# A graph attention block: crossings of the score matrices by memory instead of by TensorE

## The reference

```
u = h @ h.T / sqrt(384)                       # scores, 128 x 128, symmetric
a = softmax(u) * adjacency
attn = a / (sum(a) + 1e-10)
ctx = upper(attn) @ (h @ Wl.T + bl) + diag(attn) * (h @ Ws.T + bs) + lower(attn) @ (h @ Wr.T + br)
h = relu((ctx - mean) / sqrt(var + 1e-12) * ln_w + ln_b)
# after both layers
out = layernorm(x + h)
```

## Time and profile before

| | |
|---|---|
| median of 3 | 1630.99 us (1630.69 to 1631.91) |
| the profiled execution | 1631.82 us, of it the span of instructions 1630.1 us |
| granted TensorE clock | 0.997 of full speed |
| busy: TensorE, VectorE, GpSimd, ScalarE | 98%, 86%, 74%, 66% |
| matmuls | 9509, of them 6912 for projections, 1536 for gathers, 768 for score parts, 256 cross matmuls |
| moved by transfers | 179.17 MB, 110 GB/s |

### The profile page before, as it was taken

One profiled execution on the slowest core, in us unless ns is written; L12 is line 12 of the kernel. 1 busy time (PEld: TensorE's weight loads), 2 busy tenths in 40 slices (PEclk: granted clock), 3 DMA queues, 4 the chain that ended last, 5 costly groups with the idle time before them and its releaser, 6 DMA issues.

```text
span 1630.1 us, 35740 instructions
## 1 busy us (share of the span) xinstructions
PE 1605.1 (98%) x9509; PEld 1597.9 (98%) x9509; DVE 1398.9 (86%) x4368; ACT 1078.0 (66%) x2835; POOL 1212.5 (74%) x1542
## 2 busy tenths in 40 slices
PE   8999999999999999999999999999999999999996
PEld 7899999999999999999999999999999999999995
DVE  7788888888888888888888888888888888888886
ACT  6566666666666666666666666666666666666654
POOL 5677777777777777777777777777777777777764
PEclk9999999999999999999999999999999999999998
DMA  5444444444444444444444444444444444444431
GB/s 175 102 110 107 114 114 107 111 107 116 107 114 111 110 107 113 114 107 112 107 115 106 114 112 110 109 110 115 107 114 109 112 106 114 114 108 111 108 93 45
DMA packets 463943, 179.17 MB, mean 110 GB/s; under 512 B 348592, under 2 KB 462896, under 8 KB 463920
## 3 DMA queue, kind: packets, MB, share of 16 engines
q1 hardware_dynamic: 463920, 178.91, 43.3%
HBM read 112.92 MB, written 65.86 MB: 110 GB/s over the span
## 4 chain that ended last, share of the span: by engine, by line
PE 92%; DMA 1%; DVE 1%; SPq 1%; POOL 1%; ACT 1%; issue 1%; DVEq 0%; POOLq 0%; ACTq 0%
PE p_proj L430 70%; PE p_gather L517 16%; PE p_score L424 5%; PE p_score L446 1%; DMA rows_mem<-rows_blocks 1%; SPq L366 1%; DMA attnT_whole<-attn_mem 1%; SPq L351 0%; POOL rstd L1173 0%; POOL attnT L1163 0%; DVE stats L623 0%; POOL attnT_split L1169 0%; DVE p_gather L646 0%; DVE p_gather L619 0%; DVE rows_blocks L725 0%
## 5 line engine op out<-in xcount | busy, mean ns | idle before, releaser
L430 PE MATMUL p_proj<-w,hT_layer 128*128 128x384 f32 x6912 | 1368.6, 339 | 0.9 <-DVE w L744 0.5
L430 PEld LDWEIGHTS p_proj<-w,hT_layer 128*128 128x128 f32 x6912 | 1162.5, 188 | 2.0 <-POOL w L1220 1.0
L281 POOL TENSOR_TENSOR proj_split<-proj,proj_split 128x768 fp32r<-128x768 f32 x253 | 467.6, 1848 | 182.3 <-ACT proj_split L943 181.9
L517 PE MATMUL p_gather<-proj_split,attnT_split 128*128 128x384 f32 x1536 | 309.3, 335 | 2.3 <-POOL attnT_split L1169 1.6
L1173 POOL TENSOR_TENSOR rstd<-veps,neg_half 128x1 f32<-128x1 f32 x384 | 206.8, 549 | 91.9 <-DVE veps L632 82.6
L517 PEld LDWEIGHTS p_gather<-proj_split,attnT_split 128*128 128x128 f32 x1536 | 269.9, 188 | 4.7 <-POOL attnT_split L1169 2.7
L943 ACT ACTIVATE proj_split<-proj 128x768 fp32r<-128x768 f32 x256 | 214.9, 839 | 84.7 <-DVE proj L688 83.7
L688 DVE TENSOR_TENSOR proj<-p_proj,bias_all 128x768 f32<-128x768 f32 x256 | 244.9, 957 | 12.9 <-PE p_proj L430 5.1
L1169 POOL TENSOR_TENSOR attnT_split<-attnT,attnT_split 128x256 fp32r<-128x256 f32 x256 | 190.3, 743 | 71.0 <-ACT attnT_split L934 70.9
L947 ACT ACTIVATE o<-y,nbias,rstd 128x384 f32<-128x384 f32 x128 | 90.7, 709 | 227.0 <-POOL nbias L1177 227.0
L424 PE MATMUL p_score<-hT_layer 128*128 128x256 f32 x768 | 216.6, 283 | 1.8 <-DVE rows L720 0.8
(11 more groups left out here) (59 smaller groups left out, 1598.3 us busy)
## 6 DMA issues: line engine op xcount, KB each, us to landing
xt_raw<-xT SPq DMA_DIRECT2D x128, 192.0 KB, 2.6
xn<-x SPq DMA_DIRECT2D x128, 192.0 KB, 2.4
out<-o SPq DMA_DIRECT2D x128, 192.0 KB, 2.0
rows_mem<-rows_blocks SPq DMA_DIRECT2D x124, 192.0 KB, 1.9
rowsT<-rows_mem SPq DMA_DIRECT2D x496, 48.0 KB, 2.4
adj_layer<-adj SPq DMA_DIRECT2D x256, 64.0 KB, 1.9
attn_mem<-attn_blocks SPq DMA_DIRECT2D x124, 128.0 KB, 1.7
attnT_whole<-attn_mem SPq DMA_DIRECT2D x496, 32.0 KB, 2.2
```

Of the source, the lines that this page charges most:

```text
L281: op.tensor_tensor(proj_split[u][:, LO], proj[u][:, UP:LOW + 1, :], proj_split[u][:, HI].bitcast(F32), ALU.subtract).then_inc(s_proj_lo[k], 1)
L430: return nc.tensor.matmul(p_proj[:, which, 0:D], hT_of(k, b)[:, slot, st, c, :], w[:, k, which, mv, c, :], start=(n == 0), stop=(n == 8))
L517: last = nc.tensor.matmul(home(k, b)[:, 0:D], AT_split[u][:, st, side, :], proj_split[u][:, mv, side, :], start=(side == UP and n == 0), s ...
```

## The change

It has four parts.

1. In the loop the cross matmuls are gone. H and X of both layers are computed in one group, `pair_slice`, within `project_self(0, i)`: for graph i+2 of layer 1 and graph i-2 of layer 2. All four parts share one PSUM bank. ScalarE copies both X to SBUF in one instruction (`copy_cross`) and both H to places that are left in other banks (`keep_high`), so that the bank is free for the next pass. Layer 1's high and low input therefore has four slots instead of two, and the input is loaded a pass earlier.
2. X is transposed with the attention's trip: VectorE's `turn_cross` transposes the blocks of both X into planes 2 and 3 of `blocks`, and the trip (`store_swap`, `load_swap`) carries four planes instead of two. GpSimd adds X and its transpose (`add_cross`), right behind `attn_arrived`.
3. VectorE's `scaled_scores` take the kept H and that sum. They stand right behind `low_rows`, with a wait for `s_cross_sum` and `s_kept`, and the masks come behind layer 1's bias. The gather of layer 2 comes after the first four matmuls of layer 2's sides instead of before them. On SyncE the residual input comes ahead of `store_rows`, layer 2's adjacency behind `load_swap`.
4. The ends: graph 5's scores of layer 1 come in pass 3, with a cross matmul; graph 2's rows are transposed by TensorE; the output's mean, sum and deviation have two slots instead of one, and the last `output_squares` comes a pass earlier. In filling and closing passes the cross matmuls remain, 11 in all, as against 256 before.

The core of the diff, indented less, with empty lines left out:

```diff
+parts = [p_score[0][:, 0:2, :], p_score[0][:, 2:4, :]]
+cross_parts = p_score[0].rearrange("p (k t) n -> p k t n", t=2)[:, :, LO, :]
+E = [p_score[1][:, 0, :], p_score[1][:, 1, :]]
 p_rows = bank("p_rows", [P, 4, N])
-ident_p = [p_score[0][:, 3, :], p_score[1][:, 3, :]]
-attn_mem = [nc.dram_tensor(f"attn_mem_{slot}", (P, 2, N), F32, kind="Internal").ap() for slot in range(2)]
+ident_p = p_score[1][:, 2, :]
+kept = [p_rows[:, 3, :], p_gather[0][:, D:D + N]]
...
-def store_attn(i, slot):
-    first, last = attn_layers(i)
-    if first == 0:
-        sp.wait_ge(s_attn_blocks[0], i - 2)
-    elif last == 2:
+def store_swap(i, slot):
+    first, last = swapped(i)
+    if isinstance(i, int) and i == 3:
+        sp.wait_ge(s_blank, 1)
+        sp.wait_ge(s_attn_blocks[0], 1)
+    elif last == 4:
+        sp.wait_ge(s_cross_blocks, i - 3)
+    else:
         sp.wait_ge(s_attn_blocks[1], i - 2)
-    if first < last:
-        sp.dma_start(attn_mem[slot][:, first:last], A_blocks[:, slot, first:last]).then_inc(
-            s_attn_out[slot], 16)
-def load_attn(i, slot):
-    first, last = attn_layers(i)
-    if first == last:
-        return
-    sp.wait_ge(s_attn_out[slot], attn_moves(i, slot))
-    blocks = attn_mem[slot].rearrange("(r a) k (s b) -> s a k r b", a=B, b=B)
+    sp.dma_start(swap_mem[slot][:, first:last], blocks[:, slot, first:last]).then_inc(
+        s_swap_out[slot], 16)
+def load_swap(i, slot):
+    first, last = swapped(i)
+    sp.wait_ge(s_swap_out[slot], swap_moves(i, slot))
+    pieces = swap_mem[slot].rearrange("(r a) k (s b) -> s a k r b", a=B, b=B)
     for s in range(4):
-        sp.dma_start(AT_whole[s * B:(s + 1) * B, first:last, :].rearrange("a k (r b) -> a k r b", b=B),
-                     blocks[s][:, first:last]).then_inc(s_attn_in[slot], 16)
+        rows_s = slice(s * B, (s + 1) * B)
+        if last - first == 1:
+            sp.dma_start(whole[rows_s, first, :].rearrange("a (r b) -> a r b", b=B),
+                         pieces[s][:, first]).then_inc(s_swap_in[slot], 16)
+        else:
+            sp.dma_start(whole[rows_s, first:last, :].rearrange("a k (r b) -> a k r b", b=B),
+                         pieces[s][:, first:last]).then_inc(s_swap_in[slot], 16)
...
+elif live(i, i + 4):
+    done(sp, s_lo[0], i + 2)
+    sp.dma_start(xt_raw[:, p], xT[i + 4]).then_inc(s_xt[p], 16)
...
-if live(i, i - 1):
-    done(sp, s_attn[1], i - 3)
-    sp.dma_start(adj_tile[1][:, q], adj[i - 1]).then_inc(s_adj[1][q], 16)
+if live(i, i - 3):
+    done(sp, s_y, i - 5)
+    sp.dma_start(xn[:, q], x[i - 3]).then_inc(s_xn[q], 16)
 if live(i, i - 1) and not direct_rows(i, i - 1):
     store_rows(i - 1, q)
-store_attn(i, p)
-if live(i, i - 3):
-    done(sp, s_y, i - 5)
-    sp.dma_start(xn[:, q], x[i - 3]).then_inc(s_xn[q], 16)
+if not isinstance(i, int) or 3 <= i < G:
+    store_swap(i, p)
 if live(i, i - 1) and not direct_rows(i, i - 1):
     load_rows(i, i - 1, q)
 if closing(i) and live(i, i - 4):
     done(sp, s_side[1], i - 4)
-load_attn(i, p)
+if not isinstance(i, int) or 3 <= i < G:
+    load_swap(i, p)
+if isinstance(i, int) and i == 3:
+    done(sp, s_lo[0], 5)
+    sp.dma_start(xt_raw[:, 1], xT[7]).then_inc(s_xt[1], 16)
+if live(i, i - 1):
+    done(sp, s_attn[1], i - 3)
+    sp.dma_start(adj_tile[1][:, q], adj[i - 1]).then_inc(s_adj[1][q], 16)
 if live(i, i + 3):
...
+def pair_slice(b0, slot0, b1, slot1, n):
+    if n == 2:
+        if isinstance(b1, int) and b1 == 2:
+            done(pe, s_negmax[0], 5)
+            done(pe, s_negmax[1], 1)
+        else:
+            done(pe, s_kept, b1 - 3)
+        if b0 is not None:
+            done(pe, s_lo[0], b0)
+    if b0 is not None and 2 <= n < 2 + C:
+        step = score_step(0, b0, slot0, n - 2)
+        if n == 1 + C:
+            step.then_inc(s_parts[0], 1)
+    if n == 2 + C:
+        done(pe, s_lo[1], b1)
+    if 2 + C <= n < 2 + 2 * C:
+        step = score_step(1, b1, slot1, n - 2 - C)
+        if n == 1 + 2 * C:
+            step.then_inc(s_parts[1], 1)
...
+project_sides(0, 3, 3, 0, 2, range(18), (1, 0, 0, 3, -1), 10, 17)
 turn_attn(0, 3)
 turn_rows(1)
 gather(0, 2)
-project_self(0, 3, 1, 0, 2, (0, 4, 0))
-project_sides(1, 0, 0, 0, 3, range(18), (1, 1, 1), 8, 15)
-project_self(1, 0, 0, 0, 3)
+project_self(0, 3, 3, 0, 2, (0, 4, 0, 3, 0))
+project_sides(1, 0, 0, 0, 3, range(18), (1, 1, 1, 4, 0), 8, 15)
+project_self(1, 0, 0, 0, 3, (0, 5, 1, 4, 1), 2, 8)
+turn_rows(2)
 gather(0, 3)
...
-project_self(0, i, p, 1, i - 4)
+b0 = i + 2 if live(i, i + 2) else None
+project_sides(0, i, r, 1, i - 4, range(18))
+project_self(0, i, r, 1, i - 4, pair=(b0, (r + 2) % 4, i - 2, p))
+project_sides(1, i - 3, q, 0, i, range(4))
 gather(1, i - 4)
-project_sides(1, i - 3, q, 0, i, range(18), (1, i - 2, p))
+project_sides(1, i - 3, q, 0, i, range(4, 18))
 project_self(1, i - 3, q, 0, i)
-gather(0, i)
+gather(0, i, True)
...
-def output_mean(b):
-    done(dve, s_y_nbias, b - 1)
+                                   accum_out=y_sum[:, p:p + 1]).then_inc(s_y, 1)
+def output_mean(b, slot):
+    done(dve, s_y_nbias, b - 2)
     done(dve, s_y, b)
-    nc.vector.tensor_scalar(neg_mean[:, 2:3], y_sum[:], -1.0 / D, None,
+    nc.vector.tensor_scalar(neg_mean[:, 2 + slot:3 + slot], y_sum[:, slot:slot + 1], -1.0 / D, None,
                             ALU.mult).then_inc(s_y_mean, 1)
...
+def turn_cross(i, slot):
+    done(dve, s_crossed, i - 4)
+    if live(i, i + 2):
+        nc.vector.transpose(blocks[:, slot, 2:4].rearrange("p k n -> p (k n)"),
+                            crossed[:].rearrange("p k n -> p (k n)")).then_inc(s_cross_blocks, 1)
+    else:
+        nc.vector.transpose(blocks[:, slot, 3], crossed[:, 1]).then_inc(s_cross_blocks, 1)
...
 normalise_layer1(i - 1, q)
 low_rows(i - 2, p)
+if not isinstance(i, int) or i > 4:
+    done(dve, s_cross_sum, i - 5)
+    done(dve, s_kept, i - 5)
+    output_mean(i - 5, q)
+    if live(i, i + 1):
+        scaled_scores(0, i + 1, q, kept[0], cross_sum[:, 0])
+    scaled_scores(1, i - 3, q, kept[1], cross_sum[:, 1])
+add_bias(0, i, True)
+if live(i, i + 1):
+    mask(i, 0, i + 1, q)
 mask(i, 1, i - 3, q)
-if live(i, i + 1):
-    done(dve, s_score[0], i + 1)
+block_rows(i - 1)
 diagonal(1, i - 3, q)
 if live(i, i + 1):
-    scaled_scores(0, i + 1, q)
-add_bias(0, i, True)
-block_rows(i - 1)
-if live(i, i + 1):
-    mask(i, 0, i + 1, q)
     diagonal(0, i + 1, q)
+turn_cross(i, p)
 add_bias(0, i, False)
 row_moments(1, i - 4, p)
 row_variance(1, i - 4, p).then_inc(s_veps[1], 1)
 centre_layer2(i, i - 4)
 output_rows(i - 4, p)
-done(dve, s_score[1], i - 2)
 add_bias(1, i - 3, True)
-scaled_scores(1, i - 2, p)
-output_mean(i - 4)
 add_bias(1, i - 3, False)
...
+def copy_cross(i):
+    if live(i, i + 2):
+        done(act, s_parts[0], i + 2)
+        done(act, s_parts[1], i - 2)
+        nc.scalar.activation(crossed[:], cross_parts, ACT.Copy).then_inc(s_crossed, 1)
+    else:
+        done(act, s_parts[1], i - 2)
+        nc.scalar.activation(crossed[:, 1], cross_parts[:, 1], ACT.Copy).then_inc(s_crossed, 1)
+def keep_high(i):
+    if live(i, i + 2):
+        nc.scalar.activation(kept[0], parts[0][:, HI, :], ACT.Copy)
+    nc.scalar.activation(kept[1], parts[1][:, HI, :], ACT.Copy).then_inc(s_kept, 1)
...
 relu_rows(i, i - 2, p)
+high_rows(i - 2, p)
+exponentials(1, i - 3, q)
 if live(i, i + 1):
-    cross_scores(0, i + 1)
-high_rows(i - 2, p)
+    exponentials(0, i + 1, q)
 high_sides(1, i - 4)
 normalise_rows(i, i - 1)
-if live(i, i + 1):
-    exponentials(0, i + 1, q)
+copy_cross(i)
+high_projections(0, i)
 high_sides(0, i)
-high_projections(0, i)
-if live(i, i + 2):
-    high_input(i + 2, p)
+keep_high(i)
+if live(i, i + 3):
+    high_input(i + 3, (r + 3) % 4)
 if live(i, i + 1):
     squared_denominators(0, i + 1, q)
 squared_denominators(1, i - 3, q)
 if live(i, i - 5):
     output_squares(i - 5, q)
-cross_scores(1, i - 2)
-if live(i, i - 5):
     finish(i, q)
 high_projections(1, i - 3)
-exponentials(1, i - 2, p)
...
+def add_cross(first, last):
+    nc.gpsimd.tensor_tensor(cross_sum[:, first:last], crossed[:, first:last],
+                            whole[:, 2 + first:2 + last], ALU.add).then_inc(s_cross_sum, 1)
...
 low_projections(nc.gpsimd, pool, 1, i - 4)
 attn_arrived(i - 1, q)
+if not isinstance(i, int) or i > 4:
+    add_cross(0, 2)
 cut_sides(1, i - 4)
 deviation_layer1(i - 1)
 low_sides(1, i - 4)
...
 low_projections(nc.gpsimd, pool, 0, i)
 deviation_layer2(i - 4)
 if live(i, i - 5):
-    deviation_output(i - 5)
-if live(i, i + 2):
-    low_input(i + 2, p)
+    deviation_output(i - 5, q)
+if live(i, i + 3):
+    low_input(i + 3, (r + 3) % 4)
```

More of the change, by code:

```diff
@@ L194, in graph_block @@
         s_negmax = per_layer("s_negmax")
+        s_crossed = sem("s_crossed")
+        s_cross_blocks = sem("s_cross_blocks")
+        s_cross_sum = sem("s_cross_sum")
+        s_kept = sem("s_kept")
         s_exp = per_layer("s_exp")
@@ L254, in direct_rows, with cross_count, rows_moves, swapped @@
         def direct_rows(i, b):
```

(36 more changed lines are left out.)

247 lines of the change are left out of this document (131 added, 116 removed).

## The result

The changed kernel takes 1752.22 us (median; 1750.30 to 1753.48), the kernel before beside it 1631.45. The ratio is 1.0736, 95% interval [1.072, 1.0752]: slower by 7.4%. The profiled execution has a span of 1751.0 us. The forecast was 1748.

What follows compares the result with a forecast made beforehand. The prediction took TensorE to bound the kernel before at 12.44 us a pass; Loop A would lengthen it to 13.4, 0.96 us more over 122 passes, 117 us on 1631.0, so 1748 us, range 1665 to 1800.

Steps and rivals of the forecast that it cites:

- What bounds before: Kernel before: TensorE, busy 98% of the span with 92% of the chain, sets the pass of 12.44 us.
- The price of the removal: TensorE: two cross matmuls of 0.06 us fewer a pass, 14.8 us in all, leaving it 12.32 us a pass.
- rival 3: Both loops fall under 12.32 us, TensorE keeps the pace, and the kernel gets faster: 1615 us; chance 0.10.
- Loop A: Block_rows through the trip's landing, add_cross, scores and masks to next block_rows: 9.44 + 3.6 = 13.04 us, 13.4 with larger loads.
- The larger loads: Attention's trip: loads of 64 KB instead of 32 KB land in 2.6 us, 0.4 us more.
- Loop B: Layer 2's bias through GpSimd's low_projections, add_cross, block_rows and layer 2's rows to the same bias: 12.85 us a pass.
- rival 1: Transfers get no longer or handovers overlap better; Loop B or a Loop A of about 12.9 sets pace: 1692 us; chance 0.27.
- VectorE's own sum: VectorE's pass laid end to end, turn_cross at 0.36 included: 11.8 us with no waits, against 12.32.
- The moved issues of SyncE: SyncE's reordered loads cost nothing, up to 0.4 us if a queue issue lands in front of store_rows.
- the ends: Filling and tail: extra score matmuls and transposes, two slots for the means; put at nothing, give or take 4 us.
- The signs: Profile after: TensorE near 93% with gaps before layer 1's sides, VectorE waiting for add_cross, GpSimd for the trip's landing.
- Rival 2: Doubled store and loads get into each other and the input loads: loop 0.5 us more, pass 13.9, 1809 us; chance 0.10.

Runs made afterwards that it cites:

- before_no_cross: The kernel before with only the loop's cross matmuls left out, so the transposed low part is missing from those scores: 1604.86 us, ratio 0.9838.
- before_four: The kernel before, its attention trip carrying two more planes of zeros (store 256 KB, loads of 64 KB): 1633.79 us, ratio 1.0012.
- two_planes: The changed kernel with the trip carrying the attention alone (store 128 KB, loads of 32 KB), add_cross adding zeros: 1694.06 us, ratio 1.0384.
- flat: The changed kernel with both trips laid out plane first in device memory, so loads have three dimensions instead of four: 1649.68 us, ratio 1.012.
- act_loads: The changed kernel with the four loads of layer 1's rows issued by ScalarE instead of SyncE: 1728.97 us, ratio 1.0598.
- all_four: The changed kernel with flat, act_loads, add_cross ahead of layer 2's low projections, and ScalarE's sides copy ahead of its projections copy: 1765.24 us, ratio 1.0829.

## Why the prediction was right, step by step

**What bounds before**: right, and shown by before_no_cross. **The price of the removal**: the term was mis-sized. I read 0.06 us from the cross's start to the next start; the trace had the rest one matmul later. Two crosses are worth 0.23 us by the medians, 26.8 us were measured over the kernel, against my 14.8. The sum did not suffer, as TensorE's pace dropped out of it; rival 3 would have been 1603 instead of 1615. So the loops lost 147 us against what TensorE could have done, and gave the change a loss of 121.

**Loop A**: right in mechanism, nearly right in size. From block_rows to the landing I had 9.44 + 0.4, measured 9.95 in the pass shown and 9.89 by the median; the 64 KB loads land in 2.7 (I said 2.6). By the estimate that the prediction takes from the Trainium skill (DMA: Bandwidth & Descriptors, Anatomy of one DMA) they would have landed 0.08 us later, which the trace does not bear out for these loads: 2.2 became 2.7. From landing to block_rows I had 3.6, measured 3.4 in that pass and 3.53 by the median. The two small errors cancel: 13.4 forecast, 13.43 measured, and so close a hit is in part luck. **The larger loads** cost what they should only inside the loop, shown by before_four and two_planes.

**Loop B**: too long by 0.25 to 0.3 us: 12.85 in my sum, 12.5 by the rows of after and 12.6 by the medians of flat, as block_rows to layer 2's rows is 1.66 (I had 1.83) and add_cross to block_rows 3.46 to 3.53 (3.6). It did not touch the forecast, as loop A was the longer one by either number. The part of rival 1 in which loop A is about 12.9 is the kernel two_planes: 1694 with a pass of 12.94, where I had 1692.

**VectorE's own sum** of 11.8 never bound. turn_cross takes 0.44 us and holds the queue 0.36 as I took it. **The moved issues of SyncE** cost nothing that shows: block_rows to the issue of the store takes 0.56 us, before 0.60 (medians); **the ends** were not measured by themselves; two passes read singly (VectorE's waits end at 709.99 and 723.47) lie 13.48 us apart, near the mean of 13.43, so little is left for the ends.

**The signs**: VectorE's and GpSimd's waits came as said. TensorE's gaps did only in part: of some 1.2 us a pass, 0.3 lie before layer 1's sides, where I had put them, and the rest before layer 2's sides and before its gather, which wait for VectorE's bias and GpSimd's sides. **Two slips in the sums** moved little: a quarter of a microsecond less than 1692 is 1661 and not 1665, the lower bound of the range, and rival 3 takes off 0.8 us without a source.

**Rival 2** (collision) did not happen in the changed kernel but is real: act_loads and all_four make it happen.

## What to carry to other kernels

Before taking work off the engine that is full, write down each loop that closes over one pass, the transfers and their issues included, and compare it with the new pass: here 0.23 us came off TensorE, and a loop through memory that had about 0.7 us of slack (9.44 to the landing and 2.3 from there to the end of layer 1's rows) got 1.7 us longer by an addition, two scores, two exponentials and a larger load. Write down the neighbours of the binding loop too: opening loop A from ScalarE closed a third one 0.1 to 0.2 us below it. A transfer that is free beside the loop has its full price in it. When the loop is a queue of issues, fewer dimensions per transfer help (102 us here); a second issuing engine took only 23 us off here, as it made both trips land later and drew the rows' loads into a loop of their own.

## What the runs showed of the hardware

- A 128 column matmul with its own weights costs 115 ns in a stream of 384 column matmuls (61 behind it, 54 at the one after), where the start of the next matmul alone makes it look like 61.
- Four loads of 48 KB with four dimensions are issued in 2.58 us, four with three dimensions and the same pieces in 1.86; the 64 KB ones then land in 2.3 instead of 2.7 us. The stores of this layout, in smaller pieces, land later (256 KB in 2.3 instead of 2.0 us, 192 KB in 2.1 instead of 1.9).
- Two groups of four loads in flight from two queues land in 3.1 us each, instead of 2.5 and 2.7 in turn.
- A cross matmul of 256 columns slows the dozen matmuls behind it by some 3 ns each; open why.
